# Four PSUM banks for the attention, and split second products in two of four stages

## What is computed

```python
x = x + 0.5 * ffn(layernorm(x)); x = x + attn(layernorm(x)); x = x + 0.5 * ffn(layernorm(x))

def ffn(x):                       # 8 experts of 512 hidden units, top 2 of a softmax
    probs = softmax(x @ router_w.T); top_w, top_idx = top_k(probs, 2)
    top_w = top_w / (sum(top_w) + 1e-9)
    h = relu(einsum('tc,efc->tef', x, w1) + b1)
    y = einsum('tef,ecf->tec', h, w2) + b2
    return sum over the two chosen experts of top_w * y

def attn(x):                      # 4 heads, key width 16, value width 32
    delta = shift(x) - x
    z = tanh((x + delta * mu_x) @ W_x1.T); mus = z @ W_x2 (five of them) + x_bias
    r, w, k, v, g = projections of x + delta * mus[i]   (w through tanh and two matrices)
    S = exp(-exp(w)) * S + k v;  o = r . (S + bonus * k v)     # scan over tokens
    return (groupnorm(o) * gn_weight + gn_bias) * silu(g) @ W_o.T
```

## Time and profile before

| | us |
|---|---|
| median of 3 timed runs | 565.63 (565.23 to 566.16) |
| the profiled execution | 569.11 |
| its span in the trace | 567.3 |
| TensorE busy | 542.6 |
| VectorE busy | 301.3 |
| ScalarE busy | 226.0 |
| GpSimd busy | 188.7 |
| mean granted clock of TensorE | 0.991 |

### The profile page before, as it was taken

The page is one execution under the profiler, slowest core; times in us unless marked ns, Lnnn a source line. Parts: engine busy times, 40 slices in busy tenths (PEclk is TensorE's granted clock), DMA queues, the critical chain, the costliest instruction groups (busy, mean ns, idle before and its releaser), DMA issues.

```text
span 567.3 us, 5755 instructions
## 1 busy us (share of the span) xinstructions
PE 542.6 (96%) x1876; PEld 307.5 (54%) x1876; DVE 301.3 (53%) x625; ACT 226.0 (40%) x344; POOL 188.7 (33%) x219
## 2 busy tenths in 40 slices
PE   6899999999899999999998899999999999999996
PEld 2566666665345565645564345565645565665663
DVE  4731123534657888865566666889865554211111
ACT  2555445545044222225354244222225344444442
POOL 0012121220714766750110624766650111121122
PEclk9999999999799999999998999999999999999999
DMA  6078000120004000000001203000000004400000
GB/s 217 21 278 339 1 0 0 46 105 1 0 2 150 0 0 2 0 1 0 0 2 38 113 1 148 1 1 20 0 1 2 0 2 168 149 1 18 1 1 18
DMA packets 10206, 26.21 MB, mean 46 GB/s; under 512 B 2624, under 2 KB 2752, under 8 KB 9920
## 3 DMA queue, kind: packets, MB, share of 16 engines
q1 hardware_dynamic: 10176, 25.84, 12.6%
HBM read 24.66 MB, written 1.18 MB: 46 GB/s over the span
## 4 chain that ended last, share of the span: by engine, by line
PE 56%; issue 18%; POOL 12%; DVE 10%; DMA 2%; ACT 1%; POOLq 0%; SPq 0%; DVEq 0%; ACTq 0%
PE Y L228 25%; PE U L217 7%; PE U L219 7%; PE U L218 7%; POOL qs L877 6%; POOL xT L866 4%; DVE xnt L625 2%; PE A L293 2%; DVE bst L614 1%; PE A L306 1%; PE A L338 1%; PE A L351 1%; POOL pool_a L883 1%; POOL carry L874 1%; DVE gy L691 1%
## 5 line engine op out<-in xcount | busy, mean ns | idle before, releaser
L496 ACT ACTIVATE hid<-U,small 128x512 f32<-128x512 f32 x256 | 174.7, 687 | 265.2 <-PE U L219 264.6
L228 PE MATMUL Y<-hid,w 128*128 128x512 f32 x512 | 262.5, 596 | 2.9 <-ACT hid L496 2.8
L866 POOL TENSOR_TENSOR xT<-xT,gy 128x512 f32<-128x512 f32 x64 | 82.9, 1296 | 281.7 <-DVE gy L691 281.5
L217 PE MATMUL U<-xhi,w1lo 128*128 128x512 f32 x256 | 170.4, 666 | 0.0
L228 PEld LDWEIGHTS Y<-hid,w 128*128 128x128 f32 x512 | 96.9, 190 | 28.4 <-ACT hid L496 3.7
L691 DVE SCALAR_TENSOR_TENSOR gy<-Y,small,G 128x512 f32<-128x512 f32 x64 | 47.3, 741 | 109.4 <-PE Y L228 102.9
L219 PE MATMUL U<-xhi,w1hi 128*128 128x512 f32 x256 | 101.7, 397 | 0.0
L218 PE MATMUL U<-xlo,w1hi 128*128 128x512 f32 x256 | 101.3, 396 | 0.0
L877 POOL TENSOR_TENSOR qs<-q,pool_a 128x512 f32<-128x512 f32 x64 | 76.0, 1187 | 26.4 <-DVE pool_a L706 26.4
L217 PEld LDWEIGHTS U<-xhi,w1lo 128*128 128x128 f32 x256 | 48.6, 190 | 63.0 <-issue 59.5
L218 PEld LDWEIGHTS U<-xlo,w1hi 128*128 128x128 f32 x256 | 48.8, 191 | 40.3 <-issue 38.1
(11 more groups left out here) (114 smaller groups left out, 353.2 us busy)
## 6 DMA issues: line engine op xcount, KB each, us to landing
G<-gate_dram SPq DMA_DIRECT2D x32, 512.0 KB, 5.4
pool_a<-wexp_dram SPq DMA_DIRECT2D x8, 256.0 KB, 7.2
w<-wexp_dram SPq DMA_DIRECT2D x8, 256.0 KB, 7.2
small<-small_dram SPq DMA_DIRECT2D x1, 1104.0 KB, 9.6
qs<-const_dram SPq DMA_DIRECT2D x1, 1024.0 KB, 11.5
out_dram<-xT SPq DMA_DIRECT2D x4, 256.0 KB, 2.0
xT<-xT_dram SPq DMA_DIRECT2D x2, 256.0 KB, 4.6
gate_dram<-gate_T SPq DMA_DIRECT2D x32, 4.0 KB, 1.4
```

Source lines behind the costliest of these rows:

```text
L217: mm(dst, w1lo[:, e, f, :], xhi[:, b, :], start=True, stop=False)
L228: mm(Y[g % 2][:, :], w2[:, g % E, f, :], hid[:, n % HS, :], start=(f == 0), stop=(f == FC - 1)).then_inc(down, 1)
L496: act.activation(hid[:, n % HS, :], U[n % 3][:, :], ACT.Relu, bias=w(W_B1 + n % (E * FC), 1)).then_inc(h_f, 1)
L866: pool.tensor_tensor(dst, dst, gy[:, g % 2, :], ALU.add).then_inc(acc, 1)
```

## The change

**Banks.** `U` has two banks instead of three and the attention four (`A[0..3]`); product n of `ffn_up` waits for ReLU n - 2. The second product lags by three slots instead of two (`LAG = 3`), and the combine moves from slot 4g + 6 to 4g + 7. Mixing products rotate over four banks, spread columns over three.

**Split second products.** In stages 0 and 3, for the quarters f = 0, 1, 2 of every expert, the second product is made of three fp32r products. ScalarE runs the ReLU twice (fp32 `hid` and fp32r `hid_hi`), VectorE makes `hid_lo` by a subtraction and copies w2 of an expert into its high part, GpSimd makes w2's low part by a subtraction. They use the memory of `vhi` and `vlo`.

**Gate rows.** `G` holds five chunks of two experts in a ring, for all tiles in turn, instead of eight.

**Order.** x comes first in the queue, the weights of expert 0 ahead of x's second tile, the gates of tile 1 of stage 0 after the last inputs. The Sqrt set is loaded at the start. In the head, tile 1's second transposes, high and low parts, the logits and w1's split for expert 1 move into slots 1 to 3; routing steps of stage 0 are spread over slots 1 to 10. For the later stages logits, routing step 0 and exp of tile 0 move to the end of the stage before.

```diff
-LAG = 2
+LAG = 3
-HS, QS, SS = 5, 8, 4
+NGC = 5
+HS, HP, QS, SS = 5, 4, 8, 4
+MUS_BANK, SPREAD_BANK = (0, 3, 2, 1), (2, 0, 1)
-    return 4 * g + {0: 9, TILES - 1: 5}.get(g % TILES, 6)
+    return 4 * g + {0: 9, TILES - 1: 5}.get(g % TILES, 7)
+def in_parts(n):
+    return n // SLOTS in (0, 3) and n % FC != FC - 1
+def parts_to(n):
+    return sum(in_parts(k) for k in range(n))
...
 # SyncE
-                if s > 0:
-                    sp.wait_ge(comb, (s - 1) * TILES + (b + 1) * E)
...
                 for k in range(NQ):
-                    sp.dma_start(G[:, b, k * EQ:(k + 1) * EQ, :]...
+                    c = (s * NB + b) * NQ + k
+                    if c >= NGC:
+                        sp.wait_ge(comb, (c - NGC + 1) * EQ)
+                    sp.dma_start(G[:, c % NGC]...
+            sp.dma_start(xT[:, 0, 0, :], xi[:, 0, 0]).then_inc(x_in[0], 16)
             sp.dma_start(ident, const_in[:, C_ID:C_ID + P]).then_inc(id_l, 16)
-            sp.dma_start(xT[:, 0, 0, :], xi[:, 0, 0]).then_inc(x_in[0], 16)
             sp.dma_start(w(W_RT, W_ALL - W_RT), small_in[:, W_RT:W_ALL]).then_inc(vec_l, 16)
+            weights(0)
             sp.dma_start(xT[:, 0, 1, :], xi[:, 0, 1]).then_inc(x_in[1], 16)
-            weights(0)
...
             gates_to_rows(0, 0)
             for e in range(4, E):
                 weights(e)
-            gates_to_rows(0, 1)
...
             sp.dma_start(sel_raw, const_in[:, C_SEL:C_ALL]).then_inc(sel_l, 16)
+            gates_to_rows(0, 1)
...
 # TensorE
-                if n >= 3:
-                    pe.wait_ge(h_f, n - 2)
+                if n >= 2:
+                    pe.wait_ge(h_f, n - 1)
...
-                pe.wait_ge(h_f, n + 1)
-                mm(Y[g % 2][:, :], w2[:, g % E, f, :], hid[:, n % HS, :], start=(f == 0), stop=(f == FC - 1)).then_inc(down, 1)
+                if in_parts(n):
+                    if f == 0:
+                        pe.wait_ge(w2lo_s, g % (2 * TILES) + 1)
+                    pe.wait_ge(h_lo, parts_to(n + 1))
+                    mm(dst, w2lo[:, g % 2, f, :], hid_hi[:, n % HP, :], start=first, stop=False)
+                    mm(dst, w2hi[:, g % 2, f, :], hid_lo[:, n % HP, :], start=False, stop=False)
+                    mm(dst, w2hi[:, g % 2, f, :], hid_hi[:, n % HP, :], start=False, stop=final).then_inc(down, 1)
+                else:
+                    pe.wait_ge(h_f, n + 1)
+                    mm(dst, w2[:, g % E, f, :], hid[:, n % HS, :], start=first, stop=final).then_inc(down, 1)
...
             def mus_pair(s, h, n0):
-                if n0 < 4:
-                    pe.wait_ge(z_r, 3 * h + n0 // 2 + 2)
-                if n0 >= 2:
-                    pe.wait_ge(mterm, 10 * h + n0 - 1)
+                if n0 == 0:
+                    pe.wait_ge(z_r, 3 * h + 1)
+                    pe.wait_ge(lg_sub, NB * s + 2)
+                if n0 == 2:
+                    pe.wait_ge(z_r, 3 * h + 3)
+                if n0 >= 4:
+                    pe.wait_ge(mterm, 10 * h + n0 - 2)
...
+                if t == T_CH + 1:
+                    logits(s + 1, 0)
...
-            keep_clock(3)
-            to_channels(0, A(0, 1))
-            keep_clock(1)
-            to_channels(1, A(0, 0))
+            keep_clock(2)
+            to_channels(0, A[0])
             keep_clock(1)
...
 # ScalarE
+                if in_parts(n):
+                    if n >= HP:
+                        act.wait_ge(down, n - HP + 1)
+                    act.activation(hid[:, n % HS, :], U[n % 2][:, :], ACT.Relu, bias=bias)
+                    act.activation(hid_hi[:, n % HP, :], U[n % 2][:, :], ACT.Relu, bias=bias).then_inc(h_f, 1)
...
+                    if t == 1:
+                        ffn_hi(0, 1)
+                        split_w1(1)
+                    if t == 4:
+                        experts_exp(0, 1)
...
 # VectorE
+            def split_w2(g):
+                ...
+                if i >= 2:
+                    dve.wait_ge(down, (g - 1) * FC)
+                dve.tensor_copy(vhi[:, g % 2, :], w2[:, g % E].rearrange("p f n -> p (f n)")).then_inc(w2hi_s, 1)
+            def split_h(n):
+                if in_parts(n):
+                    dve.wait_ge(h_f, n + 1)
+                    dve.tensor_tensor(hid_lo[:, n % HP, :], hid[:, n % HS, :], hid_hi[:, n % HP, :], ALU.subtract).then_inc(h_lo, 1)
...
                     if t == 0:
                         route(0, 0, 0)
-                    if t == 1:
-                        for step in range(1, 6):
-                            route(0, 0, step)
+                    if 1 <= t < 6:
+                        route(0, 0, t)
+                    if t == 2:
+                        ffn_lo(0, 1)
+                        split_w1(1)
+                    if t == 3:
                         route(0, 1, 0)
-                    if t == 2:
-                        for step in range(1, 6):
-                            route(0, 1, step)
-                    if t % 4 == 1 and t // 4 + 2 < E:
+                    if 6 <= t < 11:
+                        route(0, 1, t - 5)
+                    if t % 4 == 2 and t // 4 + 2 < E:
                         split_w1(t // 4 + 2)
...
-                if s >= 2 and t < 6:
-                    route(s, 0, t)
-                if s >= 1 and t == 2:
-                    route(s, 1, 0)
+                if s >= 2 and t < 5:
+                    route(s, 0, t + 1)
+                if s >= 1 and (t == 5 or t == 7 or 10 <= t < 14):
+                    route(s, 1, {5: 0, 7: 1}.get(t, t - 8))
...
+                    if h is None and (t == 0 or t % FC == FC - 1):
+                        i = (t + 1) // FC
+                        if i < TILES:
+                            split_w2(s * TILES + i)
                     beside(s, h, t)
+                    split_h(n)
...
 # GpSimd
+            def split_w2(g):
+                pool.wait_ge(w2hi_s, g % (2 * TILES) + 1)
+                pool.tensor_tensor(vlo[:, g % 2, :], w2[:, g % E].rearrange("p f n -> p (f n)"), vhi[:, g % 2, :],
+                                   ALU.subtract).then_inc(w2lo_s, 1)
```

More of the change, by code:

```diff
@@ L80, in program @@
         std = sb("std", [P, 8])
+        table = sb("table", [P, 1])
         rstd = sb("rstd", [P, 8])
@@ L89, in program @@
         gate_T = sb("gate_T", [P, NB, 32])
-        G = sb("G", [P, NB, E, NT])
+        G = sb("G", [P, NGC, EQ, NT])
         hid = sb("hid", [P, HS, NT])
+        hid_hi = sb("hid_hi", [P, HP, NT], F32R)
+        hid_lo = sb("hid_lo", [P, HP, NT], F32R)
         gy = sb("gy", [P, 2, NT])
@@ L350, in out_proj @@
                     for g in range(NG):
-                        last = mm(A(s, 1 - b)[:, :], w(W_O + (g * NB + b) * P, P), o[:, g, :], start=(g == 0), stop=(g == 1))
+                        last = mm(A[3 - b][:, :], w(W_O + (g * NB + b) * P, P), o[:, g, :], start=(g == 0), stop=(g == 1))
                     last.then_inc(yp, 1)
             def beside(s, h, t):
-                if s != 1 and t == 0:
-                    logits(s, 0)
-                if t == 1:
-                    logits(s, 1)
                 if s == 0:
+                    if t == 0:
+                        logits(0, 0)
+                    if t == 1:
+                        to_channels(1, A[1])
+                    if t == 3:
+                        logits(0, 1)
                     if t == T_LN1:
@@ L368, in beside @@
                     if t == T_LN1 + 12:
-                        to_channels(LN_FFN[1] + 1, A(1, 0))
+                        to_channels(LN_FFN[1] + 1, A[1])
+                if s >= 1 and t == 1:
+                    logits(s, 1)
                 if h is None:
@@ L579, in beside @@
                 if t == SLOTS - 1:
+                    experts_exp(s + 1, 0)
                     ffn_hi(s + 1, 1)
             act.wait_ge(setup, 1)
-            for b in range(NB):
-                deviation(b)
+            act.activation(table[:, :], epsc[:, :], ACT.Sqrt)
+            deviation(0)
             split_w1(0)
-            for b in range(NB):
-                ffn_hi(0, b)
-            split_w1(1)
+            ffn_hi(0, 0)
+            deviation(1)
             act.wait_ge(vec_l, 16)
@@ L835, in _ @@
             link(dve.memset(xa[:, :, 0:1], 0.0))
[L836 to L838 removed]
+            stats(0, A[0])
             dve.wait_ge(vec_l, 16)
```

259 lines of the change are left out of this document (132 added, 127 removed).

## The result

The changed kernel takes **563.36 us** (median of 13 runs, 561.53 to 564.51), the kernel before, on the same chip, 566.16 (13 runs, 564.51 to 570.37): ratio **0.9921**, 95% interval 0.9898 to 0.9944. The forecast was 548.6. It is faster, but by 2.8 us where 17.0 were forecast, and the median lies outside the range of 539 to 558. The profiled executions stand 5.0 us apart (569.11 and 564.13), their spans 5.8 (567.3 and 561.5). The traces therefore have 5.8 us to explain, and the medians only 2.8: the profiled execution of before was 2.9 us over its median, that of after 0.8.

What follows compares the result with a forecast made beforehand. The prediction took TensorE (busy 542.6 of 567.3 us) to bound the kernel. Its terms, taken against the profile, summed to -17.0 us; off the median of 565.6 that gave 548.6 us, range 539 to 558.

Steps and rivals of the forecast that it cites:

- The four terms of attention: Stages 1 and 2: mixing products -6.4 us, entry of stage 2 -2.5, reductions -2.0, last reduction of each stage -1.5.
- the prediction's -5.8: Stage 0 from product 12 to its end: 41 split and 14 fp32 products, 40.7 us, against 46.4 before.
- a gain of 0.16 each: Stages 0 and 3: each of 96 split second products takes 0.70 us instead of 0.86, 15.4 us at most.
- Rival (d): Stages 0 and 3: the split doesn't pay, a slot stays 1.55 us, 13.5 us return, 562; chance 0.04.
- Rival (b): Attention: gains are only moved, half of 12.4 us returns, 555; chance 0.15.
- Together +0.1: Stage 3 besides its splits: entry, two banks, ReLU pairs and the wait for gates come to +0.1 us.
- No stall in the steady part: Steady slots: hid_lo is due three slots later, 0.8 to 1.9 us after it is ready, so no stall.
- rival (c): Stages 0 and 3: VectorE and GpSimd block each other, 0.65 us more in each of 30 groups, 568; chance 0.04.
- the head's +4.4: Head of stage 0: gates at about 27.3, w1(4) at 39.9, product 12 at 41.9, 4.4 us late (bounds 0 and 6).
- the first `U` starts at 12.6 us: Head of stage 0: the first `U` product starts at 12.6 us instead of 15.69.
- Rival (a): Head of stage 0 holds its gain: gates by 24 us, w1(4) by 36.6, total 543.6; chance 0.20.
- +2.7 for the tables: Stage 0: ScalarE's table loads beside ReLU pairs delay slots 48 to 50 by 2.2 us, slot 41 by 0.5.

Runs made afterwards that it cites:

- e3: The changed kernel without any split second product, banks and orders as they are: 561.27 us, ratio 0.989.
- e2: The changed kernel with the second products of the first four groups of stage 3 (16 slots) left as fp32: 557.25 us, ratio 0.9824.
- e5: The changed kernel with GpSimd's subtraction for w2's low part cut from 512 to 32 columns, except the first two groups (timing only): 557.22 us, ratio 0.9825.
- e11: The changed kernel with x's second tile issued ahead of the first weights again: 560.19 us, ratio 0.9849.
- e9: The changed kernel with the first ReLU of each pair left out in slots 40 to 55 (timing only): 562.78 us, ratio 0.9909.
- e10: The changed kernel with the subtraction hid_lo cut from 512 to 32 columns in slots 40 to 55 (timing only): 563.37 us, ratio 0.991.
- e1: The changed kernel with the weights of experts 4 and 5 issued ahead of the gates of half 0: 559.73 us, ratio 0.9861.
- e4: The changed kernel with the second products of the first four groups of stage 0 (16 slots) left as fp32: 559.88 us, ratio 0.9862.
- e12: The changed kernel, splits only in stage 0's groups 4-9, 14, 15 and stage 3 after four groups; weights 4, 5 before gates, x's second tile before first weights: 541.72 us.

## Why the prediction failed

Each term against the two traces (minus is faster):

| step | forecast | measured |
|---|---|---|
| head: product 12 later | +4.4 | **+7.6** |
| 12-16: low clock, +1.7, and three splits | +1.2 | +1.8 |
| 18 splits in 16-40 | -2.9 | -3.1 |
| 18 splits in 40-64 | -2.9 | -2.8 |
| stalls in 40-64 | +2.7 | **+4.6** |
| 64-192: attention, -12.4, and two splits | -12.7 | -12.0 |
| stage 3 entry, 192-209: 11 splits and +0.1 | -1.7 | **+3.1** |
| stage 3, 209-255: 34 splits | -5.4 | -5.4 |
| behind slot 255: three splits, one product more | +0.4 | +0.3 |

The four terms of attention are -6.4, -2.5, -2.0, -1.5. A split is put at -0.16; the product more (0.86) is the 55th against 54 in the prediction's -5.8. 40-64 grew by 1.8 us in all, and 18 splits at the 0.153 that e3 shows should have taken 2.8 off, so the stalls are 4.6. The three bold rows miss by 3.2, 1.9 and 4.8 us, 9.9 of the 11 between the forecast and the spans' -5.8. The other 3.0 us, from -5.8 to the medians' -2.8, are the two profiled executions.

Two sums in the prediction are off. The steps listed up to the gates add up to 10.0 us, which from 17.9 gives 27.9 and not 27.3, and product 12 at 42.5; and 40.7 less 46.4 is -5.7. Neither changes the outcome.

**Right.** "a gain of 0.16 each": e3 against the changed kernel gives 2.76 us for 18 splits in 16-40 and 5.22 for 34 in 209-255, 0.15 each. Rival (d) falls with that. The attention terms held in their sum, and that is partly luck. By slots the mixing products gave -8.4 (forecast -6.4), the reductions with the last ones -3.5 (-3.5), the entry of stage 2 -1.8 (-2.5); 1.8 us, which the prediction does not have, came back in slots 126 and 190 (0.9 each), to which the change moves the logits of the next stage's first tile. The mixing and the entry also rest on one execution of before, which by that estimate lost 5.1 us to the clock there, 3.4 at the mixing of stage 1 and 1.7 at the entry of stage 2. Its granted clock over the whole span was 0.991; 22 of the 41 timed executions of before beside the experiments have 0.993 or more. To take a difference against that profile off the median was a fault of the sum, part of the 3.0 us; how large a part, the runs do not show. Rival (b), which has half of it back, falls: where the clock fell in stage 1 after the change, 1.7 us came back.

**The failed step: stage 3's entry was priced as if it were steady, "Together +0.1".** "No stall in the steady part" held as it stands (16-40 and 209-255 paid in full), but I held VectorE's work for a group (3.2 in 5.75 us) against a steady slot for all of stage 3, and had costed its full order only for the head. In the entry the routing of two tiles and the first combines stand beside 13 subtractions: VectorE is busy 27.0 us of 32. The sign that I named for this, TensorE waiting for hid_lo, is what the trace shows; e2 shows its price, 4.8 us, and e5 that 2.3 of it come from GpSimd's new subtraction (its delay was counted as latency, and put at nothing here). This is rival (c)'s mechanism, at a fraction of its price and not in the steady groups where I had put it.

**The failed number: the head's +4.4.** The chain was right to the transfer, and so was its length from the first `U`: forecast 14.7 to the gates, measured 14.3; 12.6 on to w1, measured 13.2; 2.0 on to product 12, measured 2.2. What failed is "the first `U` starts at 12.6 us"; it started at 15.46: I counted x's deferred second tile as there on time, and it held TensorE 2.63 us, then the statistics that stand ahead of `ffn_lo` in VectorE's order. e11 takes this away and finds slot 0 at 12.11 and product 12 at 42.1 (forecast 41.9). Rival (a), with the gates by 24 us, falls: they came at 29.8. How late depends on the execution: e2, e9 and e10 are the changed kernel up to there and have product 12 at 43.4, 45.9 and 44.9, so 5.7 to 8.1 us late; where no low clock stood ahead of the first `U` (e1, e2, e4) it started at 13.0 to 13.8.

**The undersized term: +2.7 for the tables.** Only ScalarE's part was counted, and its 2.2 at slots 48 to 50 doesn't follow from the 7.7 us of work against 5.75 + 1.8 beside it. TensorE waited 2.0 us for hid_hi, where it did not wait before; VectorE's normalisation and routing add a wait of 1.6 for hid_lo. e9 and e10 show a part on each. Not all of it is split work: slot 51 is 0.6 longer than before in e3 and e12 too, whose groups there are whole.

## What to carry to other kernels

Here, splitting fp32 work paid on TensorE where its helpers had room (16-40, 209-255), and cost more than it gave in the three stretches where they carried routing, normalisation or table loads: list the helpers' work for every stretch with routing, normalisation or tables beside it, not for a steady slot, and leave the split out there (36 of the 96 left out, and the weights of two experts and a tile of x issued earlier, turned -2.8 us into -26).
A transfer that hangs on a computed result must not stand ahead of one that hangs on nothing: two experts' weights issued ahead of the gates brought product 12 forward by 5.4 us.
When several waits stand one behind the other, what a fix gives alone doesn't tell what it gives in a set: routing in one slot took 5.6 us off 0-16 by itself and put 2.9 on it once the weights and the early splits were out of the way. Test each member by taking it out of the set.
